# Expert tiles of 256 rows, with the gate and up weights held in the array and the rows moving

## The chip, the cores and the metric

One core of one Trainium2 chip runs the whole program in one launch. The metric is the device time of one execution in microseconds; lower is better. The kernel before was executed three times, and once more under the hardware profiler.

## The reference, cut to what matters

The input is 32 sequences of 256 tokens with 128 values each. A conditioned layer norm is followed by differential attention (16 heads of 8 + 8 values), and then by a second conditioned layer norm and a mixture of 8 experts, of which each token takes 2. The change lies in the experts alone:

```
logits = einsum('bth,eh->bte', x, router_w) + router_b
topv, topi = top_k(logits, 2)                      # 2 of 8 experts for a token
gates = softmax(topv)
for e in range(8):                                 # gate_w, up_w (8, 512, 128); down_w (8, 128, 512)
    w = sum(gates * (topi == e), -1)
    h = silu(x @ gate_w[e].T) * (x @ up_w[e].T)    # 512 inner values of a row
    out += (h @ down_w[e].T) * w
x = x + gb * out
```

## The kernel before, in words

**Attention and routing.** A software pipeline over the 32 sequences does the attention, and three sequences later the routing. For every token and each of its two experts, an indirect DMA (line 1449) writes a row of 130 words (the normalised token, the number of its pair, its weight) into `rows_sorted` in DRAM, in the region of that expert. So the 16,384 routed rows lie sorted by expert.

**Tables.** When the last sequence is routed, VectorE works out in `ffn_vector` (lines 582 to 602) where each expert's rows end, and for every tile of 128 rows its first row (`tile_row`) and the column at which its expert's weights begin (`tile_exp`). SyncE writes filler rows behind each expert's last row (lines 455 to 462): one DMA of 128 rows for each of seven experts, and one of 9 x 128 rows for the last. 16,384 rows in tiles of 128, with one begun tile for each expert but one, rounded up to a multiple of the ring of 8, are `FFN_TILES` = 136. The weights of gate and up are split into a high part (rounded to fp32r, in `wg` and `wu`) and a low part (in `wg_lo` and `wu_lo`, which lie in the memory of `kt`); the last two experts are split behind the tables (lines 604 and 605).

**The expert stage.** Four engine programs run over the tiles, each in program order, tied by semaphores (`tiles`, lines 433 to 441: the first 8 tiles written out, a hardware loop of 8 tiles per pass, the last 8 written out). For tile j:

- SyncE loads its 128 rows (line 477, a ring of 8).
- TensorE transposes the rows of tile j+1 (line 520); VectorE takes them out of PSUM as `rows_hi` (line 614) and the rest as `rows_lo` (line 616).
- TensorE multiplies with the *rows* as the stationary operand and 512 columns of weights moving, in three passes each for gate and up (line 508): high x high, high x low, low x high. The weights are addressed by the value of `tile_exp`, which a TENSOR_LOAD brings into a register (line 515). The result has rows on partitions.
- ScalarE takes silu of the gate (line 551), VectorE multiplies by up (line 621) and gives `hid`.
- TensorE transposes `hid` of tile j-1, four times 128x128 (line 532), VectorE copies that out of PSUM as `hid_t` (line 625), and TensorE multiplies `hid_t` of tile j-2 by the down weights, four products in fp32 (line 539), each of which stands in the trace as two weight loads and two matmuls.
- ScalarE scales the result by the row's weight (line 557), and GpSimd scatters it to `pair_out` in DRAM with one indirect DMA (line 647).

**The end.** `final` (from line 487) loads the two halves of each token's pair, adds them, multiplies by gb, adds the residual and stores the output.

Of the kernel before, what the change touches and what calls it, by code (L numbers as in the profile page):

```python
# [39 lines left out]
REGION = NB * SEQ + P  # L40
RING = 8
GROUP, FIN_RING = 2, 4

FFN_TILES = -(-(ROUTED // P + NE - 1) // RING) * RING
LAST_PADS = FFN_TILES - ROUTED // P + 1
SORTED_ROWS = NE * REGION + LAST_PADS * P
# [52 lines left out]
def adaln_block(nc, x, w_qk, w_v, w_o, lambdas, rms_col, router_w, router_b, gate_w, up_w, down_w,  # L99
                c_t, w_mod, max_ones, ident, mask_q, before, iota, ramp, pair_no, tile_no, filler, out):  # L100
    ctx = ExitStack()
    with ctx:
        def sb(name, shape, dt=F32):
            return ctx.enter_context(nc.sbuf_tensor(name, shape, dt))

        def ps(name, shape, dt=F32):
            return ctx.enter_context(nc.psum_tensor(name, shape, dt))
# [39 lines left out]
        wg = sb("wg", [P, NE * FF])  # L147
        wu = sb("wu", [P, NE * FF])
# [6 lines left out]
        qt = sb("qt", [P, 4, HU, SEQ], BF16)  # L155
# [18 lines left out]
        osq = sb("osq", [P, NT * NH, 2 * DH])  # L174
# [37 lines left out]
        rows_hi = sb("rows_hi", [P, 2, P], F32R)  # L212
        rows_lo = sb("rows_lo", [P, 2, P], F32R)
# [85 lines left out]
        rows_loaded = [sem(f"rows_loaded{r}") for r in range(RING)]  # L299
        row_t_ps = sem("row_t_ps")  # L300
# [6 lines left out]
        hid_t_ps = sem("hid_t_ps")  # L307
        hid_t_ready = sem("hid_t_ready")
# [65 lines left out]
        wg_lo, wu_lo = lo_weights[:, 0:NE * FF], lo_weights[:, NE * FF:2 * NE * FF]  # L374
        v_view = v[:].rearrange("p a t h k -> p (a t h k)")
        rows_in = v_view[:, 0:RING * RW].rearrange("p (r k) -> p r k", r=RING)
        act_g, hid = (ot[:, j, :, :].rearrange("p (a g) k -> p a (g k)", a=2) for j in range(2))
        hid_t = rest
        rows_out = on2[:].rearrange("p t h j d -> p (t h j d)").rearrange("p (r k) -> p r k", r=RING)
# [20 lines left out]
        p_hid_t = p_mix  # L400
        p_row_t = p_out[:, 0, 0:P]
        p_down = p_exp[:, 2, 0:DIM]
# [50 lines left out]
        def ffn_sp(sp):  # L453

            sp.wait_ge(tables, 1)
            for e in range(NE):
                start = sp.value_load(endi[0:1, e:e + 1], min_val=0, max_val=SORTED_ROWS - LAST_PADS * P)  # L457
                if e < NE - 1:
                    sp.dma_start(rows_sorted[bass.ds(start, P), :], fill[:, :]).then_inc(filled, 16)  # L459
                else:  # L460
                    sp.dma_start(rows_sorted[bass.ds(start, LAST_PADS * P), :].rearrange("(m p) r -> p m r", p=P),
                                 fill[:].unsqueeze(1).to_broadcast([P, LAST_PADS, RW])).then_inc(filled, 16)
# [7 lines left out]
            def load(j):  # L470
                if not t_active(j):
                    return
                if not (j.static and j.c < RING):

                    sp.wait_ge(pairs_stored[j.slot], 16 * j.turn)
                row = sp.value_load(tile_row[0:1, bass.ds(j.n, 1)], min_val=0, max_val=SORTED_ROWS - P)
                sp.dma_start(rows_in[:, j.slot, :], rows_sorted[bass.ds(row, P), :]).then_inc(rows_loaded[j.slot], 16)

            for c in range(RING):
                load(Tile(None, c))  # L480
            with sp.Fori(1, FFN_TILES // RING) as reg:
                for c in range(RING):
                    load(Tile(reg, c))
            for r in range(RING):
                sp.wait_ge(pairs_stored[r], 16 * (FFN_TILES // RING))
# [15 lines left out]
        def ffn_products(pe):  # L501
# [4 lines left out]
            def three_passes(to, par, hi, lo, w0):  # L506
                for k, (rows, w) in enumerate(((rows_hi, hi), (rows_hi, lo), (rows_lo, hi))):
                    m = nc.tensor.matmul(to, rows[:, par, :], w[:, bass.ds(w0, FF)].bitcast(F32R),  # L508
                                         start=(k == 0), stop=(k == 2))
                return m  # L510

            def body(j):
                j1, jt, jd = j.plus(1), j.plus(-1), j.plus(-2)
                if t_active(j):
                    w0 = pe.value_load(tile_exp[0:1, bass.ds(j.n, 1)], min_val=0, max_val=(NE - 1) * FF)
                if t_active(j1):

                    pe.wait_ge(rows_loaded[j1.slot], 16 * (j1.turn + 1))
                    t_wait(pe, row_t_ready, j1.plus(-1))
                    nc.tensor.transpose(p_row_t, rows_in[:, j1.slot, 0:DIM], idf[:]).then_inc(row_t_ps, 1)  # L520
                if t_active(j):

                    t_wait(pe, row_t_ready, j)
                    t_wait(pe, gate_done, j.plus(-2))
                    three_passes(p_gate[:, j.c % 2, :], j.c % 2, wg, wg_lo, w0).then_inc(gate_ps, 1)
                    t_wait(pe, hid_ready, j.plus(-2))
                    three_passes(p_up[:, j.c % 2, :], j.c % 2, wu, wu_lo, w0).then_inc(up_ps, 1)
                if t_active(jt):
                    t_wait(pe, hid_ready, jt)
                    t_wait(pe, hid_t_ready, jt.plus(-2))  # L530
                    for f in range(FCH):
                        m = nc.tensor.transpose(p_hid_t[:, jt.c % 2, f * P:(f + 1) * P], hid[:, jt.c % 2, f * P:(f + 1) * P], idf[:])  # L532
                    m.then_inc(hid_t_ps, 1)
# [979 lines left out]
```

## Time and profile before

| | us |
|---|---|
| median of 3 executions | 1588.82 |
| lowest and highest | 1579.2, 2478.22 |
| the profiled execution, its own time | 1589.78 |
| its span, first to last instruction | 1588.0 |
| TensorE busy | 1366.6 (86%) |
| VectorE busy | 1180.9 (74%) |
| ScalarE busy | 885.0 (56%) |
| GpSimd busy | 868.0 (55%) |

PE is TensorE, PEld its weight loads, DVE VectorE, ACT ScalarE, POOL GpSimd and SP SyncE. The busy shares are means over stages that differ: attention and routing run until about 1111 us, the tables and the last weight splits until 1125 us, the expert stage from 1127 to 1533 us, and the final additions after that. PEclk is the granted clock of TensorE as a share of its full 2.4 GHz; 0.5 is 1.2 GHz. A matmul's record is longer than the time it takes up in a stream of them, so the distance from one start to the next is what counts.

### The profile page before, as it was taken

What the parts mean: (1) busy time and instruction counts of PE and PEld (TensorE: products, weight loads), DVE (VectorE), ACT (ScalarE), POOL (GpSimd) and SP (SyncE); (2) the same over time, 40 slices, a digit from 0 to 9 for tenths busy, and PEclk for the clock granted to TensorE, in tenths of its full rate; (3) what the DMA queues carried; (4) which work ended last, traced back from release to release, by engine and by line L of the source; (5) the groups of instructions that cost most, each with busy time, mean ns of one, the idle gap of its engine ahead of it and who ended that gap; (6) DMA issues with size and microseconds to landing.
All of it is one profiled execution on the core that took longest, in us unless ns stands there. A gap on an engine that the chain in (4) does not pass through costs nothing. (4 is left out here: it accounts for less than half of the span.)

```text
span 1588.0 us, 42685 instructions
## 1 busy us (share of the span) xinstructions
PE 1366.6 (86%) x13344; PEld 1063.3 (67%) x13345; DVE 1180.9 (74%) x3082; ACT 885.0 (56%) x1918; POOL 868.0 (55%) x1279
## 2 busy tenths in 40 slices
PE   1499999999999999999999999962599999999950
PEld 1266777767777776777777676641588888888850
DVE  4567888888888888788888887866666666666647
ACT  1166777777777777777777777652133333333310
POOL 2045577677767767676776776663233333333334
PEclk9999999999999999999999999985799999999985
DMA  6433443444344354444434533300211111111139
GB/s 213 123 100 83 129 118 94 118 118 114 103 126 121 92 133 110 103 110 118 122 88 120 128 98 90 87 24 14 59 48 43 46 43 42 46 43 45 42 94 295
DMA packets 176591, 152.61 MB, mean 96 GB/s; under 512 B 21491, under 2 KB 159097, under 8 KB 176036
## 3 DMA queue, kind: packets, MB, share of 16 engines
q1 hardware_dynamic: 159096, 123.07, 30.1%
q0 software_dynamic: 8448, 16.93, 3.3%
q10 hardware_dynamic: 8880, 10.49, 1.9%
q8 instruction: 92, 1.51, 0.4%
q14 instruction: 75, 0.61, 0.1%
HBM read 89.37 MB, written 61.55 MB: 95 GB/s over the span
## 5 line engine op out<-in xcount | busy, mean ns | idle before, releaser
L988 ACT ACTIVATE probs<-p_exp 128x512 f32<-128x512 f32 x768 | 446.5, 603 | 183.6 <-PE p_exp L812 164.3
L1402 POOL TENSOR_SCALAR_AFFINE_SELECT probs<-probs 128x256 f32<-128x256 f32 (+1 forms) x768 | 365.4, 485 | 286.4 <-ACT probs L988 278.3
L1166 DVE TENSOR_REDUCE mx<-p_max 128x2 f32<-128x512 f32 x512 | 351.4, 687 | 169.9 <-PE p_max L786 168.9
L647 POOL DMA_INDIRECT pair_out<-on,v x136 | 133.6, 982 | 284.7 <-ACT on L557 279.3
L784 PE MATMUL p_max<-kt,qt 96*128 96x256 bf16 x1024 | 198.6, 275 | 40.5 <-DMA kt<-k_parts 19.7
L835 PE MATMUL p_out<-probs,v 128*32 128x256 f32 (+1 forms) x4096 | 221.0, 333 | 14.0 <-POOL probs L1402 7.5
L812 PE MATMUL p_exp<-qt,kt 100*128 100x256 bf16 x1024 | 196.7, 273 | 16.8 <-DMA qt<-max_parts 14.0
L621 DVE TENSOR_TENSOR ot<-ot,p_max 128x512 f32<-128x512 f32 x136 | 93.5, 688 | 125.8 <-PE p_max L508 106.5
L1169 DVE TENSOR_REDUCE mx<-p_max 128x4 f32<-128x512 f32 x256 | 173.2, 676 | 2.1 <-PE p_max L795 2.0
L835 PEld LDWEIGHTS p_out<-probs,v 128*32 128x32 f32 x4096 | 112.4, 109 | 85.4 <-POOL probs L1402 24.4
L1449 POOL DMA_INDIRECT rows_sorted<-h,idx x128 | 137.4, 1074 | 50.7 <-ACT probs L988 28.6
L557 ACT ACTIVATE on<-p_exp,v 128x128 f32<-128x128 f32 x136 | 50.3, 370 | 195.7 <-PE p_exp L539 195.7
L539 PE MATMUL p_exp<-wd,rest 128*128 x1088 | 143.9, 275 | 0.9 <-ACT on L557 0.9
L784 PEld LDWEIGHTS p_max<-kt,qt 96*128 96x128 bf16 x1024 | 89.3, 100 | 81.5 <-DVE mx L1166 25.6
L786 PE MATMUL p_max<-mask,idb 128*128 128x256 bf16 x512 | 141.1, 276 | 0.0
L551 ACT ACTIVATE ot<-p_exp 128x512 f32<-128x512 f32 x136 | 81.6, 600 | 95.3 <-PE p_exp L508 95.3
L539 PEld LDWEIGHTS p_exp<-wd,rest 128*128 128x128 f32 x1088 | 132.2, 192 | 1.3 <-issue 1.3
L812 PEld LDWEIGHTS p_exp<-qt,kt 100*128 100x128 bf16 x1024 | 98.6, 99 | 36.7 <-DMA qt<-max_parts 18.9
L978 ACT ACTIVATE ot<-p_out,out_scale 128x256 f32<-128x256 f32 x256 | 107.1, 475 | 0.0
L792 PE MATMUL p_max<-kt,qt 96*128 96x128 bf16 x1024 | 101.5, 222 | 4.4 <-DVE mx L1166 2.0
L1408 POOL TENSOR_TENSOR part_l<-rest,part_m 128x512 bf16<-128x512 f32 x64 | 74.2, 1160 | 51.5 <-ACT part_m L1004 51.5
L818 PEld LDWEIGHTS p_exp<-qt,kt 100*128 100x128 bf16 x1024 | 79.8, 98 | 30.8 <-issue 1.1
(169 smaller groups left out, 2757.9 us busy)
## 6 DMA issues: line engine op xcount, KB each, us to landing
qt<-q_parts SPq DMA_DIRECT2D x64, 384.0 KB
q_parts<-part_h SPq DMA_DIRECT2D x96, 128.0 KB, 2.0
kt<-k_parts SPq DMA_DIRECT2D x128, 96.0 KB
v<-rows_sorted SPq DMA_DIRECT2D x136, 65.0 KB, 1.8
q_parts<-part_m SPq DMA_DIRECT2D x64, 128.0 KB, 2.0
kt<-k_parts SPq DMA_DIRECT2D x128, 64.0 KB
qt<-pair_out SPq DMA_DIRECT2D x32, 256.0 KB, 5.4
mods<-mod_rows SPq DMA_DIRECT2D x32, 192.0 KB
```

Of the source, the lines that this page charges most:

```text
L539: m = nc.tensor.matmul(p_down, hid_t[:, jd.c % 2, f * P:(f + 1) * P], wd[:, bass.ds(w0 + f * P, P)], start=(f == 0), stop=(f == FCH - 1))
L647: nc.gpsimd.indirect_dma_start(pair_out, bass.IndirectOffsetOnAxis(rows_in[:, j.slot, DIM:DIM + 1].bitcast(U32), 0), rows_out[:, j.slot, : ...
L784: nc.tensor.matmul(p_max[:, bank, t * SEQ:(t + 1) * SEQ], qt[0:QK_ROWS, slot, h8, P:SEQ], kt[0:QK_ROWS, slot, t, h8, :], start=(t == 0), s ...
L786: m = nc.tensor.matmul(p_max[:, bank, :].rearrange("p (t k) -> p t k", t=2)[:, :, P:SEQ], idb[:], mask4[:, 0:2, :], start=False, stop=True)
L812: m = nc.tensor.matmul(p_exp[:, bank, t * SEQ:(t + 1) * SEQ], kt[0:ALL_ROWS, slot, t, h8, 0:P], qt[0:ALL_ROWS, slot, h8, :], start=True, s ...
L835: m = nc.tensor.matmul(p_out[32 * j:32 * j + 32, g % 2, SEQ - n:SEQ], v[:, b.par, tile, 2 * g + j // 2, :], src, start=(tile == 0), stop=( ...
L978: m = nc.scalar.activation(ot[:, q // 2, 2 * (q % 2) + k, :], p_out[:, k, :], ACT.Copy, scale=out_scale[:, g:g + 1])
L988: nc.scalar.activation(probs[:, g % 2, k, :], p_exp[:, k, :], ACT.Exp, scale=SCALE).then_inc(exp_done.sem, 1)
L1166: m = V.reduce_max(mx[:, w, 1, :, h8:h8 + 1].rearrange("p t o -> p (t o)"), p_max[:, bank, :].rearrange("p (t k) -> p t k", t=2), AX.X, ne ...
L1169: m = V.reduce_max(mx[:, w, 0, :, h8 - 1:h8 + 1], p_max[:, bank, :].rearrange("p (t h k) -> p t h k", t=2, h=2), AX.X, negate=True)
L1402: G.affine_select(out=blocks, in_=blocks, compare_op=ALU.is_ge, fill=zero, base=0, pattern=[[0, 2 if k < 2 else 4], [1, P]], channel_multi ...
L1449: G.indirect_dma_start(rows_sorted, bass.IndirectOffsetOnAxis(idx[:, bR.par, k:k + 1].bitcast(U32), 0), h2[:, bR.par, k // NT, k % NT, :], ...
```

## The change

A tile has 256 rows (`FT`) in place of 128, the ring has 6 places, and `FFN_TILES` becomes 72. In gate and up the two operands change places: 128x128 pieces of the *weights* are stationary and the 256 transposed rows move, so the result has inner values on partitions, which is the layout that the down product wants. The transposes of `hid` and the copy `hid_t` are gone. Because the stationary operand is now at a fixed address, the weights of a tile's expert are first copied into `w_now`, two buffers taken in turn (in the memory of `qt`): ScalarE copies the high parts of gate and up, 1024 columns, VectorE the low parts. Each tile's inner values are done in two halves, with the down product of the tile before between them. Tile fillers become 256 rows each (9 x 256 for the last expert), a load brings 256 rows, and a tile has two scatters.

```diff
-REGION = NB * SEQ + P
-RING = 8
+FT = 2 * P
+REGION = NB * SEQ + FT
+RING = 6
-FFN_TILES = -(-(ROUTED // P + NE - 1) // RING) * RING
+FFN_TILES = -(-(ROUTED // FT + NE - 1) // RING) * RING
...
@@ ffn_sp
+                pads = (FT if e < NE - 1 else LAST_PADS * FT) // P
+                sp.dma_start(rows_sorted[bass.ds(start, pads * P), :].rearrange("(m p) r -> p m r", p=P),
+                             fill[:].unsqueeze(1).to_broadcast([P, pads, RW])).then_inc(filled, 16)
...
@@ ffn_products
-            def three_passes(to, par, hi, lo, w0):
-                for k, (rows, w) in enumerate(((rows_hi, hi), (rows_hi, lo), (rows_lo, hi))):
-                    m = nc.tensor.matmul(to, rows[:, par, :], w[:, bass.ds(w0, FF)].bitcast(F32R),
-                                         start=(k == 0), stop=(k == 2))
+            def three_passes(to, par, kind, f0):
+                for f in range(2):
+                    for k, (w, rows) in enumerate(((0, rows_hi), (0, rows_lo), (1, rows_hi))):
+                        m = nc.tensor.matmul(to[:, f * FT:(f + 1) * FT], w_now[:, par, w, kind, (f0 + f) * P:(f0 + f + 1) * P],
+                                             rows[:, par, :], start=(k == 0), stop=(k == 2))
                 return m
             def body(j):
+                j1, jd = j.plus(1), j.plus(-1)
+                if t_active(j1):
+                    pe.wait_ge(rows_loaded[j1.slot], 16 * (j1.turn + 1))
+                    t_wait(pe, row_t_ready, j)
+                    for t in range(2):
+                        m = nc.tensor.transpose(p_row_t[:, t * P:(t + 1) * P], rows_in[:, j1.slot, t, 0:DIM], idf[:])
+                    m.then_inc(row_t_ps, 1)
+                for half in range(2):
+                    if t_active(j):
+                        if half == 0:
+                            t_wait(pe, row_t_ready, j)
+                            t_wait(pe, high_here, j)
+                            t_wait(pe, low_here, j)
+                        t_wait(pe, gate_done, jd, 2, half + 1)
+                        three_passes(p_gate[:, half, :], j.c % 2, 0, 2 * half).then_inc(gate_ps, 1)
+                        t_wait(pe, hid_ready, jd, 2, half + 1)
+                        three_passes(p_up[:, half, :], j.c % 2, 1, 2 * half).then_inc(up_ps, 1)
+                    if half == 0 and t_active(jd):
+                        wd0 = pe.value_load(tile_exp[0:1, bass.ds(jd.n, 1)], min_val=0, max_val=(NE - 1) * FF)
+                        t_wait(pe, hid_ready, jd, 2, 2)
+                        t_wait(pe, rows_ready, jd.plus(-2))
+                        for t in range(2):
+                            for f in range(FCH):
+                                m = nc.tensor.matmul(p_down[:, jd.c % 2, t, :], hid[jd.c % 2][:, f, t * P:(t + 1) * P],
+                                                     wd[:, bass.ds(wd0 + f * P, P)], start=(f == 0), stop=(f == FCH - 1))
+                        m.then_inc(down_ps, 1)
...
@@ ffn_activations
+            def bring_high(j):
+                    t_wait(act, up_ps, j.plus(-2), 2, 2)
+                    w0 = act.value_load(tile_exp[0:1, bass.ds(j.n, 1)], min_val=0, max_val=(NE - 1) * FF)
+                    nc.scalar.copy(w_now[:, j.c % 2, 0, :, :], w_hi[:, :, bass.ds(w0, FF)]).then_inc(high_here, 1)
...
@@ ffn_vector
+            def bring_low(j):
+                    t_wait(dve, up_ps, j.plus(-2), 2, 2)
+                    w0 = dve.value_load(tile_exp[0:1, bass.ds(j.n, 1)], min_val=0, max_val=(NE - 1) * FF)
+                    V.tensor_copy(w_now[:, j.c % 2, 1, :, :], w_lo[:, :, bass.ds(w0, FF)]).then_inc(low_here, 1)
...
-                    V.tensor_copy(hid_t[:, jt.c % 2, :], p_hid_t[:, jt.c % 2, :]).then_inc(hid_t_ready, 1)
...
@@ ffn_pool
+                for t in range(2):
+                    nc.gpsimd.indirect_dma_start(pair_out, bass.IndirectOffsetOnAxis(rows_in[:, j.slot, t, DIM:DIM + 1].bitcast(U32), 0),
+                                                 rows_out[:, j.slot, t, :], None, bounds_check=ROUTED - 1, oob_is_err=False
+                                                 ).then_inc(pairs_stored[j.slot], 16)
```

TensorE's program for one tile of 128 rows in the kernel before (names of PSUM tiles: `p_exp` holds the gate, and the down result in its third bank; `p_max` up; `p_out` the transposed rows; `p_mix` the transposed `hid`. `ot` is `hid`, `rest` is `hid_t`, `v` the loaded rows, `kt` the low weights):

```order
L515 TENSOR_LOAD tile_exp
L515 ISA x2
L520 MATMUL p_out<-idf,v 128x128 [waits row_t_ready,rows_loaded5]
L508 ISA [waits gate_done,row_t_ready]
L508 MATMUL p_exp<-wg,rows_hi 128x512
L508 REGISTER_ALU
L508 MATMUL p_exp<-kt,rows_hi 128x512
L508 MATMUL p_exp<-wg,rows_lo 128x512
L508 REGISTER_ALU [waits hid_ready]
L532 MATMUL p_mix<-idf,ot 128x128 [waits hid_t_ready,hid_ready]
L535 TENSOR_LOAD tile_exp
L539 ISA [waits rows_ready,hid_t_ready]
```

And TensorE's program for one tile of 256 rows in the changed kernel, in its own line numbers (515 gate and up, 526 the transposes of the rows, 540 and 545 the down product; the down result is now in `p_mix`, `hid` in `ot` and `rest` in turn):

```order
L526 MATMUL p_out<-idf,v 128x128 [waits row_t_ready,rows_loaded5]
L526 MATMUL p_out<-idf,v 128x128
L515 MATMUL p_exp<-rows_hi,w_now 128x256 [waits low_here,gate_done,high_here,row_t_ready]
L515 MATMUL p_exp<-rows_lo,w_now 128x256
L515 MATMUL p_exp<-rows_hi,w_now 128x256 x2
L515 MATMUL p_max<-rows_hi,w_now 128x256 [waits hid_ready]
L540 TENSOR_LOAD tile_exp
L540 ISA x2
L545 ISA [waits rows_ready,hid_ready]
L545 MATMUL p_mix<-wd,rest 128x128
L515 MATMUL p_exp<-rows_hi,w_now 128x256 [waits gate_done]
L515 MATMUL p_max<-rows_hi,w_now 128x256 [waits hid_ready]
```

Six products of 512 columns became 24 of 256, half of them ahead of the down product and half behind it; the four transposes are gone; one value is loaded into a register per 256 rows in place of four; and the down product waits for `hid_ready` of the tile just before, where it waited for a copy of the tile before that.

VectorE's program for one tile of the changed kernel (644 and 646 the rows, 654 the product of silu and up, 635 and 636 the copy of the low weights):

```order
L644 CAST rows_hi<-p_out 128x256 [waits up_ps,row_t_ps]
L646 TENSOR_TENSOR rows_lo<-p_out,rows_hi 128x256 [waits row_hi_ready]
L654 TENSOR_TENSOR rest<-ot,p_max 128x512 [waits down_ps,up_ps,gate_done]
L635 TENSOR_LOAD tile_exp [waits up_ps]
L635 ISA x2
L636 ISA
L636 COPY w_now<-kt 128x1024
L654 TENSOR_TENSOR rest<-ot,p_max 128x512 [waits down_ps,up_ps,gate_done]
```

The copy for the next tile stands between the two halves' products. On ScalarE the order of a tile is: silu of the first half, the copy of the high weights for the next tile, the two scaled copies of the down result, silu of the second half.

## Rows read from the trace of the kernel before

**Rows 1.** The page: busy time of the engines over the span.

```profile
PE 1366.6 (86%) x13344; PEld 1063.3 (67%) x13345; DVE 1180.9 (74%) x3082; ACT 885.0 (56%) x1918; POOL 868.0 (55%) x1279
```

**Rows 2.** Stretches: length; PE, PEld, DVE, ACT, POOL busy; granted clock; DMA share, GB/s.

```profile
1128.00:1140.00 12.00, 11.61 (x54) 9.63 (x55) 6.43 (x16) 2.77 (x5) 0.99 (x1) 0.73 0.14 34
1300.00:1400.00 100.00, 99.37 (x646) 86.68 (x646) 63.33 (x136) 32.96 (x68) 33.39 (x34) 1.00 0.15 43
```

**Rows 3.** Waits, 1130 to 1550 us: who for whom, total, times, longest.

```profile
ACT on L557 <- PE p_exp L539: 195.7, 136, 1.5
PEld p_out L520 <- issue: 4.9, 14, 0.5
```

**Rows 4.** Groups of instructions, 1130 to 1550 us: count, busy us, mean ns, idle before.

```profile
L621 DVE TENSOR_TENSOR ot<-ot,p_max 128x512 f32<-128x512 f32 x136 | 93.5, 688 | 125.8 <-PE p_max L508 106.5 <-ACT ot L551 18.4 <-issue 0.9
L551 ACT ACTIVATE ot<-p_exp 128x512 f32<-128x512 f32 x136 | 81.6, 600 | 95.3 <-PE p_exp L508 95.3
L557 ACT ACTIVATE on<-p_exp,v 128x128 f32<-128x128 f32 x136 | 50.3, 370 | 195.7 <-PE p_exp L539 195.7
L614 DVE CAST rows_hi<-p_out 128x128 fp32r<-128x128 f32 x134 | 39.1, 292 | 16.6 <-PE p_out L520 7.1
```

**Rows 5.** Timeline of weight loads and matmuls: start, length, instruction, count.

```profile
1219.76 0.19 PEld L508 LDWEIGHTS p_exp<-wg,rows_hi 128*128 128x128 f32 x1
1219.87 0.19 PEld L508 LDWEIGHTS p_exp<-kt,rows_hi 128*128 128x128 f32 x1
1221.03 0.59 PEld L532 LDWEIGHTS p_mix<-idf,ot 128*128 128x128 f32 x4
...
1220.10 0.39 PE L508 MATMUL p_exp<-kt,rows_hi 128*128 x1
1221.02 0.39 PE L508 MATMUL p_max<-wu,rows_lo 128*128 x1
```

**Rows 6.** The same timeline, around one down product and the tile behind it.

```profile
1242.27 0.97 PEld L539 LDWEIGHTS p_exp<-wd,rest 128*128 128x128 f32 x8
1244.65 0.40 PE L508 MATMUL p_max<-wu,rows_lo 128*128 x1
1245.14 0.69 DVE L621 TENSOR_TENSOR ot<-ot,p_max 128x512 f32<-128x512 f32 x1 [0.94 <-PE p_max L508]
```

**Rows 7.** The same of attention: fp32 loads with 8 columns moving, bf16 with 256.

```profile
614.96 0.52 PEld L928 LDWEIGHTS p_mix<-rw,h2t 128*128 128x128 f32 x4 [0.20 <-issue]
615.65 0.21 PEld L812 LDWEIGHTS p_exp<-qt,kt 100*128 100x128 bf16 x2
```

**Rows 8.** ScalarE's timeline, line 557: one tile, and the seventh and eighth behind it.

```profile
1196.19 0.37 ACT L557 ACTIVATE on<-p_exp,v 128x128 f32<-128x128 f32 x1 [1.44 <-PE p_exp L539]
...
1216.96 0.37 ACT L557 ACTIVATE on<-p_exp,v 128x128 f32<-128x128 f32 x1 [1.42 <-PE p_exp L539]
1219.81 0.37 ACT L557 ACTIVATE on<-p_exp,v 128x128 f32<-128x128 f32 x1 [1.42 <-PE p_exp L539]
```

**Rows 9.** Timeline: last fillers, first load, first and last work of the stage.

```profile
1119.87 0.38 SPq L461 DMA_DIRECT2D rows_sorted<-fill  x1
1125.05 0.38 SPq L477 DMA_DIRECT2D v<-rows_sorted  x1
1127.15 0.45 PE L520 MATMUL p_out<-idf,v 128*128 128x128 f32 x1 [17.22 <-DMA v<-rows_sorted]
1128.51 0.79 PE L508 MATMUL p_exp<-wg,rows_hi 128*128 x1
1531.50 1.15 PE L539 MATMUL p_exp<-wd,rest 128*128 x8 [0.65 <-ACT on L557]
```

**Rows 10.** Copies from SBUF to SBUF: VectorE (1110 to 1126 us), ScalarE (200 to 1000 us).

```profile
L387 DVE CAST kt<-wg 128x512 fp32r<-128x512 f32 x2 | 0.8, 424 | 0.0
L1004 ACT CAST part_m<-rest 128x512 bf16<-128x512 f32 x52 | 31.8, 612 | 0.0
```

**Rows 11.** DMA queues over 1175 to 1505 us, all there are; packets, MB, share.

```profile
q1 hardware_dynamic: 16128, 7.46, 9.6%
q0 software_dynamic: 3583, 7.10, 6.2%
```

More of the change, by code:

```diff
@@ L104, in sb, with shared @@
             return ctx.enter_context(nc.sbuf_tensor(name, shape, dt))
+        def shared(first, second):
+            with nc.sbuf_tensor(*first) as a:
+                pass
+            return a, sb(*second)
         def ps(name, shape, dt=F32):
@@ L146, in adaln_block @@
         mrow = sb("mrow", [NB, 4, DIM])
-        wg = sb("wg", [P, NE * FF])
-        wu = sb("wu", [P, NE * FF])
+        w_hi = sb("w_hi", [P, 2, NE * FF])
+        wg, wu = (w_hi[:, k, :] for k in range(2))
         wd = sb("wd", [P, NE * FF])
         xres = sb("xres", [P, TILES * DIM])
-        qt = sb("qt", [P, 4, HU, SEQ], BF16)
+        qt, w_now = shared(("qt", [P, 4, HU, SEQ], BF16), ("w_now", [P, 2, 2, 2, FF], F32R))
         kt = sb("kt", [P, 4, 2, HU, SEQ], BF16)
@@ L211, in adaln_block @@
         fill = sb("fill", [P, RW])
-        rows_hi = sb("rows_hi", [P, 2, P], F32R)
-        rows_lo = sb("rows_lo", [P, 2, P], F32R)
+        rows_hi = sb("rows_hi", [P, 2, FT], F32R)
         tile_row = sb("tile_row", [P, FFN_TILES], I32)
@@ L473, in load, with body @@
                 if not (j.static and j.c < RING):
[L475 to L483, printed above, removed]
+                    sp.wait_ge(pairs_stored[j.slot], 32 * j.turn)
+                row = sp.value_load(tile_row[0:1, bass.ds(j.n, 1)], min_val=0, max_val=SORTED_ROWS - FT)
+                sp.dma_start(rows_in[:, j.slot, :, :], rows_sorted[bass.ds(row, FT), :].rearrange("(t p) r -> p t r", p=P)
+                             ).then_inc(rows_loaded[j.slot], 16)
+            def body(j):
+                load(j.plus(2))
+            load(Tile(None, 0))
+            tiles(sp, body)
             for r in range(RING):
-                sp.wait_ge(pairs_stored[r], 16 * (FFN_TILES // RING))
+                sp.wait_ge(pairs_stored[r], 32 * (FFN_TILES // RING))
             def final(g):
@@ new lines, in ffn_activations @@
+            act.wait_ge(w_split, SPLIT_STEPS)
+            act.wait_ge(tables, TABLE_STEPS)
+            def body(j):
+                j1, jd = j.plus(1), j.plus(-1)
+                if not t_active(j):
+                    bring_high(j1)
+                for half in range(2):
+                    if t_active(j):
+                        t_wait(act, gate_ps, j, 2, half + 1)
+                        t_wait(act, hid_ready, jd, 2, half + 1)
+                        nc.scalar.activation(act_g[:, half, :], p_gate[:, half, :], ACT.Silu).then_inc(gate_done, 1)
+                    if half == 0 and t_active(j):
+                        bring_high(j1)
+                    if half == 0 and t_active(jd):
+                        t_wait(act, down_ps, jd)
+                        if not (jd.static and jd.c < RING):
+                            act.wait_ge(pairs_stored[jd.slot], 32 * jd.turn)
+                        for t in range(2):
+                            m = nc.scalar.activation(rows_out[:, jd.slot, t, :], p_down[:, jd.c % 2, t, :], ACT.Copy,
+                                                     scale=rows_in[:, jd.slot, t, DIM + 1:DIM + 2])
+                        m.then_inc(rows_ready, 1)
```

106 lines of the change are left out of this document (35 added, 71 removed).

## The prediction

> **What bounds the kernel now.** I read the page first for the shares of the engines [rows 1], then the busy time by stretch. A mean of 86% for TensorE says little; in the expert stage, 1300 to 1400 us, it is busy 99.37 of 100 us at full granted clock, while VectorE has 63, ScalarE 33 and GpSimd 33 [rows 2]. The waits of the stage say the same from the other side: ScalarE waits 195.7 us for the down product, and TensorE for nothing but 14 short pauses of its own issue [rows 3]. So whatever takes TensorE time off an expert tile shortens the kernel, until another engine's chain becomes longer, and the attention stage does not matter here.
>
> How long a tile takes, on TensorE, from starts and not from records: a pass of 512 columns is (1221.02 - 1220.10) / 4 = 0.230 us [rows 5]. Four transposes and the following down product: the four loads span 0.59 us with the last 0.14 to 0.19 long, 0.11 us apiece [rows 5], and the eight loads of a down product are (0.97 - 0.19) / 7 = 0.111 us apart [rows 6]. One transpose of rows, 6 passes, 4 transposes, 8 loads and matmuls: 0.11 + 1.38 + 0.44 + 0.89 = 2.82 us. Two neighbouring tiles are 2.85 us apart, but eight tiles take 1219.81 - 1196.19 = 23.62 us, 0.8 us more than eight times 2.85 [rows 8]: TensorE's instruction stream, with two register loads per tile, runs dry now and then. The whole stage, from the first transpose to the end of the last down product, is 1531.50 + 1.15 - 1127.15 = 405.5 us for 136 tiles [rows 9].
>
> **The change part by part, per tile of 256 rows.**
>
> Transposes of the rows: two, 0.22 us, as before.
>
> Transposes of the inner values: eight per 256 rows go, 0.87 us. VectorE's two copies of them go as well; it was not the bound.
>
> Down product: 16 loads and matmuls, 16 x 0.111 = 1.78 us, as before for as many rows.
>
> Gate and up: twelve passes of 512 columns (12 x 0.230 = 2.77 us) become 24 of 256 columns, each with a new stationary operand. The trace has no fp32r pass of 256 columns. From below: no pair of a full load and a matmul in it comes faster than 0.11 us. The fp32 loads in front of matmuls of only 8 columns are (0.52 - 0.19) / 3 = 0.11 us apart, so that is what a load of 128 columns takes up; two bf16 pairs of 256 columns take 0.21 us with their tail [rows 7]. The first two fp32r loads of a tile, where nothing is in their way, are also 0.11 us apart [rows 5]. This gives 24 x 0.111 = 2.66 us. From above, inside the forecast: 512 columns at 2.4 GHz are 0.213 us and take 0.230, and if those 0.017 us belong to the instruction and not to the column, 256 columns take 0.107 + 0.017 = 0.124 us, and 24 of them 2.98 us. I take half of a pass of 512, 0.1155 us and 2.77 us, since it is the same kind of product and lies between the two.
>
> Sum of TensorE: 0.22 + 2.77 + 1.78 = **4.77 us** (4.66 to 4.98), where 256 rows took 5.7 to 5.9 us.
>
> Number of tiles: 72 x 256 = 18,432 rows in place of 136 x 128 = 17,408; the sum below counts 72.
>
> The copies into `w_now` are work for two engines that have room. VectorE: 512 columns from SBUF to SBUF take 0.42 us, so 1024 between 0.7 and 0.85 us [rows 10]; with rows_hi and rows_lo of 256 columns (0.29 us for 128 and 0.69 for 512, so 0.42 each) and two products of 0.69 us [rows 4] it has about 3.0 of 4.77 us. ScalarE: 512 columns take 0.61 us, so 1024 at most 1.22 [rows 10]; with two silus of 0.60 and two copies of 0.37 [rows 4] at most 3.2 us. Both are counted at nothing, hidden by TensorE. Behind the ScalarE copy stand the scaled down results, which are not due before the down product ends, some 3.6 us into the tile; the copy is over at about 3.0. If that cover were gone, up to 1.2 us per tile would lie open.
>
> The wait that is new: the down product of tile j-1 needs both halves of `hid`, the second of which starts only when the last up pass of j-1 has run. From the end of that pass to the start of the product on VectorE it is 1245.14 - (1244.65 + 0.23) = 0.26 us [rows 6]; with 0.69 us for the product and some 0.1 us for the signal back this is 1.05 us. The cover is the two transposes and twelve passes ahead of the down product, 0.22 + 1.39 = 1.61 us. So it is hidden by 0.5 us.
>
> Register loads: one in place of four, far from its use, and 42 pairs of load and matmul against 38. I expect much of the 0.8 us per loop pass to go; at worst it stays for each of 10 passes, 8 us, at best it is nothing. I take the middle, 4 us.
>
> Start and end: before the first gate pass there are now 256-column takes (0.26 us more) and VectorE's copy, so 1128.51 - 1127.15 = 1.36 us [rows 9] becomes about 2.6. The first 6 to 7 us of the stage run at the low level of 1.2 GHz, 0.73 being the mean clock of the first 12 us [rows 2]; that costs 3 us as before. The last tile's down product stands alone behind its `hid`, 1 us. With 0.4 us for the very end that makes 7.0 us. The last filler DMA (9 x 128 rows) was issued at 1119.87 and the first load at 1125.05 [rows 9]; twice the rows cost between 0 and 5 us more, and I take 3, for a transfer that is partly fixed. The last tile's second scatter adds 1 us.
>
> Stage: 72 x 4.77 + 7.0 + 4.0 = 354.4 us against 405.5, so -51.1; with the 3 and the 1 it is -47.1 us. The profiled execution's own time was 1589.78 us, one above the median of 1588.82, so the sum gives **1543 us**. With the lower ends (0.111 us, no pauses, no filler cost) it is 1528, with the upper (0.124 us, 8 us of pauses, 5 for the filler) 1564.
>
> **The rivals.**
>
> *The loads are not hidden.* In gate and up the stationary operand now changes for every 256 columns. If an fp32r load could not run under the matmul before it, a pair would take 0.111 + 0.107 = 0.218 us, a tile 0.22 + 5.23 + 1.78 = 7.23 us, the stage 72 x 7.23 + 11 = 532, and the kernel 1589.8 + 532 - 405.5 + 4 = 1720 us, slower. It decides from a pair of about 0.142 us on, where 72 tiles of 5.4 us fill the old stage. Against it: the down product streams its columns (two passes of 128 for each fp32 load) and loads in the same 0.111 us [rows 6], and the fp32r loads have the same 0.19 us records as those loads [rows 5]. The Trainium skill has a rule that speaks for it: TensorE: Matmul & The Clock Gate, Part 3, "The mechanism", says that a weight load overlaps running matmuls only when its row group differs. By that rule the sum would be the one of this rival; the rows of the down product, with all 128 rows in use, contradict it. I leave it 5%.
>
> *A chain of the other engines becomes the bound.* If ScalarE's second silu comes late (it stands behind the scaled copies) or VectorE's copy stretches, the 0.5 us of slack at the down product is used up. The mechanism costs what exceeds it; at 0.3 us per tile 72 x 0.3 = 22 us and 1565 us. For it: three engines now pass each half around within one tile, where a full tile lay between before. Against it: VectorE and ScalarE have over 1.5 us to spare per tile. 13%.
>
> *The loop is fetched anew on each pass.* Between 1175 and 1505 us only two queues move, none with instructions [rows 11], so eight tiles of the old program, 304 loads and matmuls, stay in reach. The new loop has 6 x 84 = 504 and its other instructions on top. If each of the 10 branches back must wait some 2 us, as long as a load of rows takes from issue to use [rows 9], that is 20 us and 1563 us. The Trainium skill, Runtime: NRT & Kernel Launch, "Instruction fetch mechanics", has such a rule: a taken branch to a target outside a window of two pages of 256 instructions stalls for the fetch; the same section gives TensorE's buffer as 2048 instructions, which would hold the loop. No row here shows a loop of that size. 5%.
>
> **How the numbers follow.** The forecast has 77%, and its own range is 1528 to 1564. The serial loads have 5% at 1720, the chain 13% around 1565 (1550 to 1590), the fetch 5% at 1563. The range of 1526 to 1578 us takes in the forecast's bounds and most of the second and third, and leaves out the serial loads. What a measurement of this kernel tells from no change is about 2%, or 32 us: faster means under 1557. Of the forecast, the part above 1557 needs both the dear pass and most of the pauses, about a sixth: 0.64 remain, and 0.03 from the rivals, so faster 0.67; same 0.26; slower 0.07, the serial loads and the far end of the chain.
>
> **What would show it.** Right: starts of neighbouring gate passes 0.111 to 0.124 us apart, tiles 4.7 to 5.0 us apart, TensorE without a wait for VectorE in the stage, a stage of 345 to 375 us, and the first load of rows no later than 1130 us. Wrong: a distance of 0.2 us between passes (the first rival), a wait of the down product for `hid` (the second), packets of an instruction queue inside the loop (the third), or a granted clock that falls inside the stage because TensorE waits.

## The result, and the profile after

| | before | changed |
|---|---|---|
| median of 4 executions, us | 1587.91 | 1545.01 |
| lowest to highest, us | 1579.2 to 2478.22 | 1540.07 to 1546.98 |
| ratio to before, 95% interval | | 0.9731 [0.9701, 0.9760] |
| span of the profiled execution, us | 1588.0 | 1543.4 |
| expert stage, first transpose to the end of the last down product, us | 405.5 | 357.2 |

The change is faster by 2.7%; forecast were 1543 us and a stage of 354.4 us. The one execution of 2478.22 us stands apart from all others: the ratio leaves it out, the median of 4 still counts it. The page of the changed kernel, its busy times and the chain that ended last:

```profile
span 1543.4 us, 41532 instructions
PE 1307.1 (85%) x13658; PEld 1068.2 (69%) x13785; DVE 1136.2 (74%) x2899; ACT 957.8 (62%) x2007; POOL 875.8 (57%) x1287
PE p_mix L545 8%; PE p_exp L515 7%; PE p_max L515 7%; PE p_out L526 1%; DMA probs<-mod_rows 1%; SPq L498 1%; DMA rows_sorted<-fill 0%; SPq L501 0%; POOL rows_sorted L1482 0%; DVE probs L667 0%; POOL probs L693 0%; SPq L464 0%; DVE kt L398 0%; SPq L466 0%; DMA v<-rows_sorted 0%
```

The shares of the page hardly moved from [rows 1], but for ScalarE, 56 to 62%. The same stretch as in [rows 2], with its columns:

```profile
1300.00:1400.00 100.00, 100.00 (x863) 100.00 (x863) 57.31 (x102) 58.52 (x103) 39.55 (x41) 1.00 0.19 51
```

TensorE is now busy without a gap, and in its weight loads too (86.68 us of 100 before). The latter says little by itself: the record of a load is 0.19 us long, so loads 0.118 us apart overlap in it. ScalarE went from 33 to 59 us, and VectorE from 63 to 57. The timeline of weight loads within one tile (start, length, instruction), as [rows 5] showed it of before:

```profile
1251.46 0.19 PEld L515 LDWEIGHTS p_exp<-rows_hi,w_now 128*128 128x128 f32 x1
1251.58 0.19 PEld L515 LDWEIGHTS p_exp<-rows_lo,w_now 128*128 128x128 f32 x1
1251.70 0.30 PEld L515 LDWEIGHTS p_exp<-rows_hi,w_now 128*128 128x128 f32 x2
...
1252.76 0.19 PEld L515 LDWEIGHTS p_max<-rows_hi,w_now 128*128 128x128 f32 x1
```

Twelve loads start within 1252.76 - 1251.46 = 1.30 us, eleven steps of 0.118 us. So the load of the next 128x128 piece does run under the 256 columns of the one before. The groups of the stage, 1120 to 1505 us, that answer to [rows 4] and price what [rows 10] only bounded (count, busy us, mean ns, idle before):

```profile
L570 ACT ACTIVATE ot<-p_exp 128x512 f32<-128x512 f32 x144 | 86.1, 598 | 90.9 <-PE p_exp L515 85.8
L557 ACT CAST w_now<-w_hi 128x1024 fp32r x72 | 75.3, 1046 | 23.0 <-issue 15.3 <-PE p_max L515 2.0
L636 DVE CAST w_now<-kt 128x1024 fp32r x72 | 50.0, 695 | 10.8 <-issue 4.8
L579 ACT ACTIVATE probs<-p_mix,v 128x128 f32<-128x128 f32 x144 | 45.0, 363 | 58.2 <-PE p_mix L545 58.2
L644 DVE CAST rows_hi<-p_out 128x256 fp32r<-128x256 f32 x72 | 30.1, 418 | 8.7 <-PE p_out L526 8.7
```

The copies take 1.05 us on ScalarE and 0.70 on VectorE. Who waits for whom, 1130 to 1490 us (total, times, longest), beside [rows 3]:

```profile
ACT probs L579 <- PE p_mix L545: 58.2, 72, 3.1
PE p_out L526 <- DVE rows_lo L646: 1.1, 1, 1.1
PE p_mix L545 <- DVE rest L654: 0.9, 1, 0.9
PE p_exp L515 <- DVE w_now L636: 0.6, 1, 0.6
```

TensorE waits three times in the whole stage, at its first tiles and its last; the 14 pauses of issue of [rows 3] are gone. The beginning and the end, as in [rows 9]:

```profile
1117.46 0.37 SPq L466 DMA_DIRECT2D rows_sorted<-fill  x1
...
1125.78 1.57 SPq L482 DMA_DIRECT2D v<-rows_sorted  x2
...
1128.08 0.66 PE L526 MATMUL p_out<-idf,v 128*128 128x128 f32 x2 [20.82 <-DMA v<-rows_sorted]
...
1483.28 2.05 PE L545 MATMUL p_mix<-wd,rest 128*128 x16 [0.92 <-DVE rest L654]
```

The stage runs from 1128.08 to 1485.33 us, 357.2 us. And the DMA queues between 1175 and 1450 us, beside [rows 11]:

```profile
q1 hardware_dynamic: 15504, 7.59, 11.4%
q0 software_dynamic: 3584, 6.78, 7.9%
q8 instruction: 1, 0.02, 0.0%
```

### The profile page after: what moved, and what is told of

It reads as the page before. It is cut to its first block and busy times, and to the rows that moved or that the text cites. A ratio compares the mean times of both kernels' runs of the same rounds, so it can differ in the third digit from the quotient of the medians.

```text
span 1543.4 us, 41532 instructions
## 1 busy us (share of the span) xinstructions
PE 1307.1 (85%) x13658; PEld 1068.2 (69%) x13785; DVE 1136.2 (74%) x2899; ACT 957.8 (62%) x2007; POOL 875.8 (57%) x1287
## 5 line engine op out<-in xcount | busy, mean ns | idle before, releaser
L680 POOL DMA_INDIRECT pair_out<-probs,v x144 | 141.5, 983 | 233.8 <-ACT probs L579 207.0
L570 ACT ACTIVATE ot<-p_exp 128x512 f32<-128x512 f32 x144 | 86.1, 598 | 90.9 <-PE p_exp L515 85.8
L515 PE MATMUL p_exp<-rows_hi,w_now 128*128 128x256 f32 x576 | 140.0, 305 | 0.6 <-DVE w_now L636 0.6
L515 PE MATMUL p_max<-rows_hi,w_now 128*128 128x256 f32 x576 | 127.5, 283 | 0.0
L851 PE MATMUL p_exp<-qt,kt 100*128 100x128 bf16 x1024 | 99.4, 219 | 7.1
L515 PEld LDWEIGHTS p_exp<-rows_hi,w_now 128*128 128x128 f32 x576 | 100.0, 191 | 1.0 <-issue 1.0
```

The lines of the kernel that those rows point to most:

```text
L515: m = nc.tensor.matmul(to[:, f * FT:(f + 1) * FT], w_now[:, par, w, kind, (f0 + f) * P:(f0 + f + 1) * P], rows[:, par, :], start=(k == 0), ...
L680: nc.gpsimd.indirect_dma_start(pair_out, bass.IndirectOffsetOnAxis(rows_in[:, j.slot, t, DIM:DIM + 1].bitcast(U32), 0), rows_out[:, j.slot ...
L851: m = nc.tensor.matmul(p_exp[:, bank, c:c + P], kt[0:ALL_ROWS, slot, t, h8 - 1 + hh, P:SEQ], qt[0:ALL_ROWS, slot, h8 - 1 + hh, P:SEQ], sta ...
```

## The experiments

Attention ends some microseconds earlier or later from one execution to the next, and the stage began between 1123 and 1145 us in these runs. So beside the median (with that of the kernel before on the same chip) each run has its stage, first transpose to end of the last down product in its trace, and that is the finer measure: the changed kernel and the three runs that leave its tiles as dear as they were (after_regs, after_act_copies, after_fill) lie between 356.5 and 357.2 us.

| run | median us | before, same chip | ratio, 95% | stage us |
|---|---|---|---|---|
| changed kernel | 1545.01 | 1587.91 | 0.9731 [0.9701, 0.9760] | 357.2 |
| after_tr | 1609.67 | 1588.15 | 1.0117 [1.0069, 1.0164] | 420.0 |
| before_1tr | 1587.46 | 1588.15 | 1.0003 [0.9981, 1.0025] | 404.3 |
| before_144 | 1613.92 | 1588.15 | 1.0143 [1.0102, 1.0184] | 428.3 |
| after_down_first | 1656.67 | 1588.15 | 1.0427 [1.0386, 1.0468] | 468.5 |
| after_narrow | 1534.50 | 1591.25 | 0.9663 [0.9610, 0.9716] | 344.9 |
| after_regs | 1544.80 | 1591.25 | 0.9711 [0.9659, 0.9764] | 357.1 |
| after_act_copies | 1545.14 | 1591.25 | 0.9722 [0.9662, 0.9783] | 356.5 |
| after_fill | 1556.52 | 1595.52 | 0.9748 [0.9722, 0.9774] | 357.0 |
| after_71 | 1548.76 | 1595.52 | 0.9708 [0.9687, 0.9729] | 352.3 |
| before_1ld | 1573.75 | 1593.58 | 0.9865 [0.9820, 0.9911] | 389.5 |
| before_1tr_1ld | 1536.62 | 1593.58 | 0.9659 [0.9625, 0.9693] | 351.3 |
| down_first_silu | 1616.08 | 1593.58 | 1.0149 [1.0116, 1.0182] | 426.4 |

**The transposes, put back into the changed kernel.**

```diff
                         t_wait(pe, rows_ready, jd.plus(-2))
+                        for t in range(2):
+                            for f in range(FCH):
+                                nc.tensor.transpose(p_mix[:, jd.c % 2, SEQ + t * P:SEQ + (t + 1) * P],
+                                                    hid[jd.c % 2][:, f, t * P:(t + 1) * P], idf[:])
```

> The changed kernel, with the eight 128x128 transposes of the inner values per tile of 256 rows put back ahead of the down product; their results go to an unused part of a PSUM tile and nobody reads them. Theory (TensorE's own time is the whole of an expert tile): 8 x 0.109 = 0.87 us per tile of 4.88, 72 tiles, +63 us, so about 1608 us. Rival (much of the gain came from fewer register loads and shorter waits, and the transposes were partly covered): under +30 us, below 1575 us.

The stage grew by 62.7 us, 0.109 us for each of 576 transposes: the theory to the digit. In the changed kernel TensorE sets the pace, and work put into it comes out in full. That it is the array and not the instruction stream is shown by after_regs below.

**The transposes, taken out of the kernel before.**

```diff
-                    for f in range(FCH):
+                    for f in range(1):
                         m = nc.tensor.transpose(p_hid_t[:, jt.c % 2, f * P:(f + 1) * P], hid[:, jt.c % 2, f * P:(f + 1) * P], idf[:])
```

> The kernel before, with one transpose of the inner values per tile in place of four; three quarters of the transposed values are stale. Everything else stands. Theory (TensorE's own time): 3 x 0.109 x 136 = -44 us, about 1544 us: the removed transposes alone are worth the measured gain. Rival (the kernel before is also held by TensorE's instruction issue, two register loads per 2.85 us): TensorE starts to pause more and at most -20 us shows, 1568 us or more.

Next to nothing: 404.3 against 405.5 us. This refuted my theory of the kernel before. The waits of this run, 1140 to 1500 us, where those of [rows 3] had 4.9 us in 14 pauses:

```profile
PEld p_out L520 <- issue: 28.5, 100, 0.7
PE p_out L520 <- issue: 8.1, 20, 0.5
```

TensorE pauses at the head of nearly every tile, on nothing that the profile shows but its own instruction stream. From one transpose of rows (line 520) to the next, no tile between 1200 and 1300 us is shorter than 2.83 us, though its work in the array fell to 2.50 by the sum. The new theory: an old tile has two bounds side by side, 2.82 us of the array and a stream of instructions at least as long. A view of line 515 in the trace of the kernel before, 1219 to 1223 us (count, ns least/median/most, first and last start), shows what fills the stream:

```profile
L515 PEldq FUSED_REGOPS  x2: 151/151/151, 1219.1 to 1222.4; - x2
L515 PEldq SEQ_ASSERT  x2: 18/18/18, 1219.3 to 1222.7; - x2
L515 PEldq TENSOR_LOAD <-tile_exp x1: 310/310/310, 1222.0 to 1222.0; - x1
```

One value brought into a register and checked keeps the stream from 1222.0 to 1222.7 us, and an old tile does it twice, beside some eight smaller register operations for the addresses of its weights. In both kernels one tile of each eight takes 3.34 to 3.38 us, the others 2.83 to 3.08: once per loop pass the stream falls behind, perhaps at the branch, which no run tests.

**One register load less, alone and with the transposes.**

```diff
                 if t_active(jd):
-                    w0 = pe.value_load(tile_exp[0:1, bass.ds(jd.n, 1)], min_val=0, max_val=(NE - 1) * FF)
+                    if not t_active(j):
+                        w0 = pe.value_load(tile_exp[0:1, bass.ds(jd.n, 1)], min_val=0, max_val=(NE - 1) * FF)
```

> The kernel before with one register load of TensorE per tile in place of two: the down product takes its weights by the offset loaded for the gate of the tile two further on, so a few tiles at the border of two experts use the wrong down weights. Theory (an old tile has two bounds that lie side by side: 2.82 us of loads and passes in the array, and an instruction stream of about 2.85 us with two register loads): the array holds the tile alone now, (2.95 - 2.83) x 136 = -16 us, about 1572 us. Rival (the stream of instructions is no bound, and the one transpose kept in the run with three fewer was held by another chain): no change, within 4 us.

> Both edits: the kernel before with one transpose of the inner values per tile in place of four (three quarters of them stale) and one register load in place of two. Theory (two bounds side by side): each edit alone gives 0 and -16 us, and both together (2.95 - 2.50) x 136 = -61 us, about 1527 us. Rival (another chain, such as the one over hid and its copy, holds the tile near 2.85 us): no more than -16 us, 1572 us.

Stage: -16.0 us for the load alone, as expected, and -54.2 us for both, where the theory had -61 and the rival -16. The two edits give 0 / -1.2 / -16.0 / -54.2 us (neither, transposes, load, both): neither is worth what both are. With one load less every tile between 1200 and 1300 us takes 2.82 to 2.84 us, the array's sum. With both edits most take 2.49 to 2.53 us, but two of each eight 2.60 to 2.66. These two make up most of the missing 7 us; what holds them was not tested. Otherwise TensorE is busy throughout again (the stretch 1300 to 1400 us; before_1tr above, both below):

```profile
1300.00:1400.00 100.00, 97.01 (x544) 77.86 (x543) 62.32 (x135) 32.78 (x68) 33.39 (x34) 1.00 0.16 44
```

```profile
1300.00:1400.00 100.00, 100.00 (x633) 87.02 (x632) 69.97 (x158) 37.66 (x78) 38.90 (x40) 1.00 0.19 50
```

**Register loads added to the changed kernel**, one `pe.value_load` of `tile_exp` at the head of each half.

> The changed kernel with two more loads of a value into a register of TensorE per tile, one ahead of each half's gate passes; the values are not used. Theory (the pauses of the kernel before came from its instruction stream being just in time with two such loads per 2.85 us; with three per 4.88 us there is room): at most +4 us, under 1549 us. Rival (each load holds up the passes behind it by part of its 0.3 to 0.75 us): 2 x 0.3 x 72 = +43 us or more.

No change, 357.1 us: with three loads in a tile of 4.88 us the stream still keeps ahead, so it is the array that holds the tile. The changed kernel has one.

**The filler rows alone**, `FFN_TILES = 144` in the kernel before.

> The kernel before with 144 tiles of 128 rows in place of 136 (the eight more hold filler rows, and the last filler transfer has 17 x 128 rows in place of 9 x 128), so as many rows as the changed kernel goes through. Theory: 8 x 2.95 = +23.6 us and 0 to 5 us for the filler, 1612 to 1617 us: what the coarser tiles cost by themselves. Rival (filler tiles are cheaper than others, since their scatter writes nothing): under +18 us.

The stage grew by 22.8 us, 2.85 us a tile, where the mean tile has 2.95: a tile of filler costs nearly what any tile costs. The filler transfer lies ahead of the stage. From its issue to the first load of rows it is 7.9 us here (1122.95 to 1130.80) against 5.2, +2.7 us. The median ratio says +22.7 us, with an interval of 16 to 29 us, too wide to show that.

**The down product ahead of both halves.** The block under `if half == 0 and t_active(jd)` was moved up, ahead of `for half in range(2)`.

> The changed kernel with the down product of the tile before moved ahead of the first half's gate and up passes, directly behind the two transposes. Theory: the second half of hid is there 1.05 us after the last up pass, and only 0.22 us of transposes cover it now, so TensorE waits about 0.8 us per tile, 72 x 0.8 = +58 us, about 1603 us. Rival (the hid chain is shorter than I worked out, or the wait is taken up elsewhere): under +30 us.

The stage grew by 111 us, twice the forecast. ScalarE's timeline over one tile shows why (line 570 silu, 557 the copy, 579 the down results):

```profile
1251.20 0.60 ACT L570 ACTIVATE ot<-p_exp 128x512 f32<-128x512 f32 x1 [3.86 <-PE p_exp L515]
1252.00 1.05 ACT L557 CAST w_now<-w_hi 128x1024 fp32r x1 [0.20 <-PE p_max L515]
1252.95 0.62 ACT L579 ACTIVATE probs<-p_mix,v 128x128 f32<-128x128 f32 x2
1253.46 0.60 ACT L570 ACTIVATE ot<-p_exp 128x512 f32<-128x512 f32 x1
```

The two halves' gates now follow each other at once, and the second silu stands behind a copy and two scaled results. So that order was changed too:

```diff
                         nc.scalar.activation(act_g[:, half, :], p_gate[:, half, :], ACT.Silu).then_inc(gate_done, 1)
-                    if half == 0 and t_active(j):
-                        bring_high(j1)
-                    if half == 0 and t_active(jd):
...
+                if t_active(j):
+                    bring_high(j1)
+                if t_active(jd):
...
```

So the silus of both halves come first, then the copy, then the scaled results.

> The changed kernel with the down product ahead of both halves, as in the earlier run, and with ScalarE's order changed to suit it: both silus first, then the copy of the high weights, then the two scaled copies. Theory (of the 111 us that the early down product cost, 58 are the missing cover of the hid chain and the rest is ScalarE's copies standing ahead of the second silu): the wait falls from 1.5 to 0.8 us per tile, about 1603 us. Rival (the whole 111 us come with the place of the down product): still above 1640 us.

Stage 426.4 us, 69 above the changed kernel. The waits at the down product, 1200 to 1500 us, of the first run and of this one:

```profile
PEld p_mix L534 <- issue: 71.5, 46, 1.7
```

```profile
PEld p_mix L534 <- issue: 48.8, 51, 1.1
```

1.55 us and 0.96 us per tile; times 72 that is 112 and 69 us, the two growths. So 42 us were ScalarE's order, and 69 the cover, where I had said 58. The timelines price the chain itself. In this last run (1250 to 1257 us) VectorE's product ends at 1255.96, the down product's first matmul starts 0.14 us later, and the last up pass had started at 1254.88:

```profile
1254.88 0.28 PE L515 MATMUL p_max<-rows_hi,w_now 128*128 128x256 f32 x1
1255.28 0.68 DVE L654 TENSOR_TENSOR ot<-ot,p_max 128x512 f32<-128x512 f32 x1
1256.10 1.15 PE L534 MATMUL p_mix<-wd,ot 128*128 x8 [0.72 <-DVE ot L654]
```

From the end of that pass (1254.88 + 0.12) it is 1.10 us, where I had 1.05. In the changed kernel (1250 to 1256 us) the product ends at 1253.94 and the down product starts at 1254.63:

```profile
1253.25 0.69 DVE L654 TENSOR_TENSOR ot<-ot,p_max 128x512 f32<-128x512 f32 x1 [1.66 <-PE p_max L515]
1254.63 1.61 PE L545 MATMUL p_mix<-wd,ot 128*128 x13
```

Of these 0.69 us the signal takes 0.14, so 0.55 us are to spare (0.54 to 0.60 in the tiles from 1200 to 1260 us).

**Both copies on ScalarE.**

```diff
 nc.scalar.copy(w_now[:, j.c % 2, 0, :, :], w_hi[:, :, bass.ds(w0, FF)]).then_inc(high_here, 1)
+nc.scalar.copy(w_now[:, j.c % 2, 1, :, :], w_lo[:, :, bass.ds(w0, FF)]).then_inc(low_here, 1)
...
-                    w0 = dve.value_load(tile_exp[0:1, bass.ds(j.n, 1)], min_val=0, max_val=(NE - 1) * FF)
-                    V.tensor_copy(w_now[:, j.c % 2, 1, :, :], w_lo[:, :, bass.ds(w0, FF)]).then_inc(low_here, 1)
+                    return
```

> The changed kernel with both copies into w_now on ScalarE, high then low; VectorE copies none. Theory (ScalarE has room): 1.05 us more, 4.1 of 4.88 us busy; the down results start about 0.3 us later and the second silu with them, inside the 0.5 to 0.6 us of slack at the down product: +0 to +5 us. Rival (the chain of the other engines is close to being the bound): the second silu is late by 0.5 us or more beyond the slack, 72 x 0.5 = +36 us.

No change, 356.5 us: ScalarE has room for the second copy. It doesn't even use up slack at the down product: VectorE's product still ends 0.69 to 0.73 us ahead of it, where I had expected 0.3 us less.

**Passes of half the width.**

```diff
-                        m = nc.tensor.matmul(to[:, f * FT:(f + 1) * FT], w_now[:, par, w, kind, (f0 + f) * P:(f0 + f + 1) * P],
-                                             rows[:, par, :], start=(k == 0), stop=(k == 2))
+                        m = nc.tensor.matmul(to[:, f * FT:f * FT + P], w_now[:, par, w, kind, (f0 + f) * P:(f0 + f + 1) * P],
+                                             rows[:, par, 0:P], start=(k == 0), stop=(k == 2))
```

> The changed kernel with only the first 128 of the 256 transposed rows moving in each gate and up pass; the other half of the inner values is stale. The weight loads stay. Theory (a pass of 256 columns is already about as short as the load under it): passes come 0.110 us apart in place of 0.118, -0.2 us per tile, 72 tiles, -14 us, about 1531 us. Rival (the moving columns set the pace and loads are cheap): passes of about 0.06 us, -1.4 us per tile, -100 us, until another engine's chain holds the tile. Third possibility: fp32r with 128 columns streams slower per column, and the time rises.

The stage shrank by 12.3 us, 0.007 us per pass. Its weight loads:

```profile
1250.52 0.19 PEld L515 LDWEIGHTS p_exp<-rows_hi,w_now 128*128 128x128 f32 x1
1250.63 0.19 PEld L515 LDWEIGHTS p_exp<-rows_lo,w_now 128*128 128x128 f32 x1
1250.74 0.30 PEld L515 LDWEIGHTS p_exp<-rows_hi,w_now 128*128 128x128 f32 x2
```

Half the columns, and the distance goes only from 0.118 to 0.11 us: about the distance of the fp32 loads with 8 columns in [rows 7]. That an fp32r pass of 128 columns would stream at a slower rate and so also end at 0.11 us is not excluded by this run.

**The large filler first.** `for e in (NE - 1, *range(NE - 1))` in `ffn_sp`.

> The changed kernel with the filler of the last expert (9 x 256 rows, one large DMA) issued first of the eight and not last. Theory (the first load of rows waits for this transfer): it now lands while the other seven are issued, the first load goes out 4 to 5 us earlier, -4.5 us, about 1540.5 us. Rival (the weight split on VectorE or the scatters of the last sequence hold the start as well): -1 us or nothing.

No gain. From the first filler's issue to the first load of rows it takes 1142.73 - 1125.58 = 17.2 us here, and 1125.78 - 1109.39 = 16.4 us in the changed kernel. The fillers' issue and landing (count, KB each, us), here and in the changed kernel:

```profile
rows_sorted<-fill SPq DMA_DIRECT2D x1, 1170.0 KB, 9.0
rows_sorted<-fill SPq DMA_DIRECT2D x7, 130.0 KB, 6.7
```

```profile
rows_sorted<-fill SPq DMA_DIRECT2D x1, 1170.0 KB, 7.5
rows_sorted<-fill SPq DMA_DIRECT2D x7, 130.0 KB, 2.3
```

The seven small ones now land after 6.7 us in place of 2.3, and the large one after 9.0 in place of 7.5. This fits small ones that queue behind the large one, which was not tested by itself. My theory was wrong, and for another reason than the rival's.

**71 tiles**, with that filler order; tile 72 is left out on every engine.

> As the kernel with the large filler first, and with 71 tiles in place of 72, the most that 16,384 rows of 8 experts can need. Theory: one tile of 4.88 us less, and 8 x 256 filler rows: -9.5 us against the changed kernel, about 1535.5 us. Rival (the tail of the last tile is set by the scatters and not by TensorE): only -5 us.

The stage is 4.7 us shorter than with 72, one tile; the other half of the -9.5 us forecast was the filler order, which had brought nothing. The ratio is 0.9708 against 0.9748 on the same chip, with intervals that just overlap. It is the best complete kernel here by the stage; by the medians its interval overlaps that of the changed kernel, which ran on another chip.

## Why the prediction was right

**The bound after the change: right.** TensorE's array sets the pace, without a gap, and time put into it comes out in full (after_tr).

**The bound before the change: half right.** "TensorE's instruction stream, with two register loads per tile, runs dry now and then" was the true sign of a second bound, but I took it for 0.8 us per eight tiles and its removal for 4 us. It was as long as the array's work: taking transposes out alone gave nothing. That this did no harm to the sum is luck in part: it set new tiles, counted from the array, against the measured 405.5 us of the old stage, in which the second bound is contained; and the change takes both away, eight transposes and three of four register loads per 256 rows. Whether the stream would hold a new tile that kept all four loads I had not worked out. Three still fit (after_regs); four were not tried.

**Transposes, 0.87 us per 256 rows: right** (0.109 us each in after_tr), and needed together with the loads of values.

**Gate and up: 0.118 us a pass, 0.1155 taken.** It lies within 0.111 to 0.124. Twelve passes of 512 columns cost 2.77 us before, 24 of 256 now 2.83 us: the change of operands costs 0.06 us and removes what comes behind. One reading behind the lower bound was wrong: that no pair of a full load and a matmul comes faster than 0.11 us in the trace of the kernel before. It holds for its full fp32 loads only. Three bf16 loads of 128x128 ahead of matmuls of 8 columns start within 0.05 us:

```profile
589.96 0.10 PEld L946 LDWEIGHTS p_mix<-both,onesb 128*128 128x128 bf16 x1
589.99 0.12 PEld L948 LDWEIGHTS p_mix<-both,onesb 128*128 128x128 bf16 x2
```

So the bf16 pairs of [rows 7] show what 256 columns take and not what a load does, and the bound stood on the fp32 loads alone; after_narrow, at 0.11 us, bears it out.

**The tile: 4.77 forecast, 4.88 measured.** (From first transpose to first transpose, the mean of 61 tiles between 1150 and 1450 us; 72 of them leave 6 us of the stage for start and end.) Half of the 0.11 us is the passes; the other 0.05 us must lie where one kind of matmul follows another, such as the 0.13 us from the last load of a half (1252.76) to the next transpose (1252.89). The 0.11 us are +7.9 us over the stage; the pauses were 0 in place of 4, and start and end 6 in place of 7, with a granted clock of 0.70 over 1128 to 1140 us where [rows 2] has 0.73. Together 357.2 in place of 354.4.

**Filler: 3 us taken.** From the last filler's issue to the first load it is 8.3 us, before 5.2 [rows 9]: +3.1. Behind the stage the changed kernel has 58.1 us and the old one 55.3; I had +1 there. The new stage also began 0.9 us later. -48.3 + 0.9 + 2.8 is the -44.6 us between the spans, where the forecast had -47.1. Three misses cancel in part, and that is luck: the stage is 2.8 us longer than forecast. The time behind it grew by 1.8 us more than forecast: from the end of the stage to the first load of pairs it is now 5.0 us (1485.33 to 1490.31) in place of 3.5 (1532.65 to 1536.11), and where the other 1.3 us of the 2.8 lie no run shows. The stage began 2.1 us earlier than forecast, because the first filler went out at 1109.39 and not at 1112.05 us, within what attention varies by.

**The copies at nothing: right**, with room for both on one engine. **The new wait at the down product: hidden, with 0.55 us to spare** where I had 0.5. But its cover is more than the passes ahead of it: the down product between the halves also gives ScalarE time for its copies. I had priced that at up to 1.2 us per tile and not joined it to this wait; it was 42 us of the 111 in after_down_first.

**Serial loads (5%): no.** Such a pair would take 0.218 us; it takes 0.118. The Trainium skill's rule (TensorE: Matmul & The Clock Gate, Part 3, "The mechanism"), that a load overlaps running matmuls only with another row group, does not hold for these pairs, all with 128 rows in use. The same section also says that a load into the background weight buffer is pulled ahead of running matmuls; the 0.118 us agree with that, though no run here shows such a buffer.

**The loop fetched anew (5%): no.** One instruction packet in 275 us, and no pause at the branch. The Trainium skill (Runtime: NRT & Kernel Launch, "Instruction fetch mechanics") gives a window of two pages beyond which a branch stalls; the loop's 504 loads and matmuls with their register operations showed no such stall, which agrees with the buffer of 2048 instructions in the same section.

**What the coarser tiles cost:** 8 more tiles of the old size are 22.8 us (before_144). The gain of 48.3 us in the stage is net of that.

## What to carry to other kernels

Before pricing the removal of work from a busy engine, add up its instruction stream too: a short "issue" wait at a tile's head can mean that a second bound stands beside the first, and only removing both pays in full (-1, -16 and -54 us here). Swapping stationary and moving operands of a product, so that its result has the layout of the next product, cost 0.06 us and saved 0.87 us of transposes per tile, as long as the moving side has 256 columns to run over each new load. Where a product is put between two halves to cover a wait, look which other engine's work uses the same gap.

## What the hardware showed that I had not expected

- A value loaded into a TensorE register and checked occupies its instruction stream for about 0.7 us (0.31 and 0.15 us records with gaps between). Two of them in a tile, beside its smaller register operations, kept tiles from coming closer than 2.83 us.
- An fp32r pass takes 0.230 us for 512 columns, 0.118 for 256 and 0.11 for 128, always with a full weight load: from 256 columns to 128 next to nothing is gained.
- Among three bf16 loads of 128x128 with 8 columns moving each followed the last after 0.02 to 0.03 us, fp32 ones after 0.11.
- Small filler transfers issued behind a large one landed after 6.7 us (median) in place of 2.3.
